# Norm floors taken as a maximum over stored pairs, and unread transposes at four places of the first two batches

## What is computed

```python
EPS = 1e-12
def l2norm(t):
    n = norm(t);  return t / maximum(n, EPS)
def tanh_norm(t):
    n = norm(t);  return tanh(n) * (t / maximum(n, EPS))
q, k, v = l2norm(q), l2norm(k), l2norm(v)
attn = square(relu(q @ k.T))
out  = tanh_norm(attn @ v)
x    = x + out @ Wout
```

## Time and profile before

| | us |
|---|---|
| median of 3 runs | 552.65 (552.19 to 552.93) |
| the profiled execution | 551.87, of which span of the core 549.8 |
| TensorE busy | 527.1 (96%) |
| VectorE busy | 425.2 (77%) |
| ScalarE busy | 371.4 (68%) |
| GpSimd busy | 331.3 (60%) |

### The profile page before, as it was taken

One profiled execution on the slowest core, in us unless ns is written; L12 is line 12 of the kernel. 1 busy time (PEld: TensorE's weight loads), 2 busy tenths in 40 slices (PEclk: granted clock), 3 DMA queues, 4 the chain that ended last, 5 costly groups with the idle time before them and its releaser, 6 DMA issues.

```text
span 549.8 us, 10227 instructions
## 1 busy us (share of the span) xinstructions
PE 527.1 (96%) x3288; PEld 393.9 (72%) x3288; DVE 425.2 (77%) x1004; ACT 371.4 (68%) x682; POOL 331.3 (60%) x280
## 2 busy tenths in 40 slices
PE   8798899999999999898999999999999999999997
PEld 7565557676767666686878878878868878878884
DVE  5877868888978698669769778778769778777765
ACT  5697859687769786644565865865865865755654
POOL 6645919393947584395466655655655655665562
PEclk9899989999999999999999999999999999999999
DMA  7401010101010100660291760870760780771930
GB/s 218 131 2 30 1 30 1 32 1 30 2 31 1 30 2 9 171 148 2 77 209 30 184 153 4 176 156 11 184 151 4 182 175 5 170 159 35 214 83 20
DMA packets 37253, 44.75 MB, mean 81 GB/s; under 512 B 5840, under 2 KB 20304, under 8 KB 37200
## 3 DMA queue, kind: packets, MB, share of 16 engines
q1 hardware_dynamic: 32512, 42.40, 33.3%
q10 hardware_dynamic: 4688, 1.71, 1.3%
HBM read 40.94 MB, written 3.15 MB: 80 GB/s over the span
## 4 chain that ended last, share of the span: by engine, by line
PE 61%; POOL 14%; issue 13%; DVE 6%; ACT 4%; DMA 1%; SPq 0%; POOLq 0%; ACTq 0%; DVEq 0%
PE PS L1245 59%; POOL hl L517 11%; DVE aT L892 2%; ACT v L556 1%; POOL sr L446 1%; ACT rl L581 1%; DMA Osb<-wa_dram 1%; DVE n L871 1%; POOL mrstd L508 1%; POOL rstd L461 1%; DVE nmx L904 1%; ACT sqv L563 0%; POOL fxl L468 0%; DVE hb L1118 0%; PE PS L1338 0%
## 5 line engine op out<-in xcount | busy, mean ns | idle before, releaser
L517 POOL TENSOR_TENSOR hl<-hb,hh 128x512 fp32r<-128x512 f32 x127 | 164.3, 1295 | 129.2 <-ACT hh L735 124.9
L728 ACT ACTIVATE sil<-PS 128x512 f32<-128x512 f32 (+1 forms) x136 | 80.8, 595 | 79.0 <-PE PS L1245 72.4
L1113 DVE TENSOR_TENSOR PS<-sil,PS 128x512 f32<-128x512 f32 x128 | 88.3, 690 | 54.3 <-PE PS L1245 33.0
L1245 PE MATMUL PS<-fxh,wfh 128*128 128x512 f32 x264 | 104.9, 397 | 3.3 <-DVE hb L1118 2.9
L735 ACT ACTIVATE hh<-hb 128x512 fp32r<-128x512 f32 x128 | 80.3, 627 | 35.3 <-DVE hb L1118 33.4
L1245 PE MATMUL PS<-fxl,wfh 128*128 128x512 f32 x264 | 104.1, 394 | 0.0
L1245 PE MATMUL PS<-fxh,wfl 128*128 128x512 f32 x264 | 103.7, 393 | 0.0
L1118 DVE TENSOR_TENSOR hb<-PS,wbc 128x512 f32<-128x512 f32 x128 | 88.5, 691 | 12.9 <-issue 4.2
L892 DVE SCALAR_TENSOR_TENSOR aT<-PS,rl 128x1024 f32<-128x1024 f32 x64 | 75.2, 1216 | 14.7 <-ACT rl L581 14.6
L581 ACT ACTIVATE rl<-PS 128x1024 f32<-128x1024 f32 x64 | 62.8, 1050 | 21.7 <-PE PS L1245 21.7
L436 POOL TENSOR_TENSOR sr<-n2o,half 128x32 f32<-128x32 f32 x7 | 37.9, 5414 | 44.4 <-DVE n2o L899 44.4
(11 more groups left out here) (182 smaller groups left out, 900.1 us busy)
## 6 DMA issues: line engine op xcount, KB each, us to landing
wbc<-w_dram SPq DMA_DIRECT2D x48, 512.0 KB, 11.7
wbc<-w_dram SPq DMA_DIRECT2D x32, 128.0 KB, 3.0
wbc<-w_dram SPq DMA_DIRECT2D x16, 256.0 KB, 4.2
wfs<-wf_dram SPq DMA_DIRECT2D x32, 98.0 KB, 2.2
band_dram<-zero SPq DMA_DIRECT2D x16, 80.0 KB, 1.7
band<-band_dram ACTq DMA_DIRECT2D x4, 320.0 KB, 3.0
X<-x_dram SPq DMA_DIRECT2D x1, 896.0 KB, 8.2
Osb<-wa_dram SPq DMA_DIRECT2D x3, 256.0 KB, 3.8
```

The lines of the kernel that those rows point to most:

```text
L517: g.tensor_tensor(hl[:, n % RING, :], hb[:, n % RING, :], hh[:, n % RING, :].bitcast(F32), ALU.subtract).then_inc(F("hl"), 1)
L728: s.activation(sil[0:rows, n % 2, :], PS[0:rows, G0 + n % 2, :], ACT.Silu).then_inc(F("silu"), 1)
L1113: v_.tensor_tensor(PS[:, bank, :], sil[:, n % 2, :], PS[:, bank, :], ALU.mult).then_inc(F("t"), 1)
L1245: return nc.tensor.matmul(o, w, m, start=start, stop=stop)
```

## The change

Two parts.

First, n2 and nn get a last dimension of 2. GpSimd stores the floor in both places once at the start (two memsets, 576 and 64 elements in each partition); afterwards every sum is written to place 0, and place 1 keeps the floor. The maximum with the floor is then a reduction (maximum) over the innermost pair where it was a tensor_scalar with a constant. This holds for L882, L904, L1012 and L1017. The first reader, `value_norms(0,0)`, waits for the memsets.

Second, a new helper `fill_idle(times, job)` waits until the PSUM bank of the named coming job is free and writes `times` unread transposes of the identity to it. It is called at four places: 6 ahead of `score(0)` (bank of `g 0 2`), 10 ahead of `score(1)` (bank of `qk 1 0`), 8 ahead of `score(5)` (bank of `qk 2 0`), and 10 ahead of `score(9)` (bank of `F 0 0`).

```diff
-            n2 = ab("n2", [P, 3, 2, 3 * H])
+            n2 = ab("n2", [P, 3, 2, 3 * H, 2])
...
-            nn = ab("nn", [P, 2, H])
+            nn = ab("nn", [P, 2, H, 2])
...
             g.memset(ind[:, :, :], 0.0).then_inc(cs("ind0"), 1)
+            g.memset(n2[:, :, :, :, :], NORM_EPS * NORM_EPS).then_inc(cs("floors"), 1)
+            g.memset(nn[:, :, :, :], NORM_EPS).then_inc(cs("floors"), 1)
             inverse_deviation(0)
...
-                g.tensor_tensor(nn[:, :, :], sr[:, :, :], rr[:, q % 3, :, 0:H], ALU.mult).then_inc(A("n"), 1)
+                g.tensor_tensor(nn[:, :, :, 0], sr[:, :, :], rr[:, q % 3, :, 0:H], ALU.mult).then_inc(A("n"), 1)
...
             def value_norms(n, t):
                 dve.wait_ge(A("sqv"), 2 * n + t + 1)
-                v_.tensor_reduce(n2[:, n % 3, t, 2 * H:3 * H], sqv[:, :].rearrange("p (h d) -> p h d", d=DV),
+                if n == 0 and t == 0:
+                    dve.wait_ge(cs("floors"), 2)
+                v_.tensor_reduce(n2[:, n % 3, t, 2 * H:3 * H, 0], sqv[:, :].rearrange("p (h d) -> p h d", d=DV),
                                  AX.X, ALU.add).then_inc(A("n2v"), 1)
...
-                v_.tensor_scalar(nm[:, n % 3, t, :], n2[:, n % 3, t, :], NORM_EPS * NORM_EPS, None, ALU.max).then_inc(A("nm"), 1)
+                v_.tensor_reduce(nm[:, n % 3, t, :], n2[:, n % 3, t, :, :], AX.X, ALU.max).then_inc(A("nm"), 1)
...
-                v_.tensor_scalar(nmx[:, :, :], nn[:, :, :], NORM_EPS, None, ALU.max).then_inc(A("nmx"), 1)
+                v_.tensor_reduce(nmx[:, :, :], nn[:, :, :, :], AX.X, ALU.max).then_inc(A("nmx"), 1)
...
+            def fill_idle(times, *job):
+                bank, k = turns.at[job]
+                after(pe, Z(f"free{bank}"), k - 1)
+                for _ in range(times):
+                    nc.tensor.transpose(PS[:, bank, 0:P], ident[:, :], ident[:, :])
+
...
             group(0, 1)
+            fill_idle(6, "g", 0, 2)
             score(0)
...
+                if b < 2:
+                    fill_idle(10 if b == 0 else 8, "qk", n, 0)
                 if b != 2:
                     score(NG * b + 1)
...
                 if b == 1:
+                    fill_idle(10, "F", q, 0)
                     score(NG * n + 1)
```

More of the change, by code:

```diff
@@ L217, in hybrid_layer @@
         ld = Sems(ctx, nc, "in_x0 in_x in_wv0 in_wv1 in_wq in_wp in_wo in_wf0 in_wf1 in_wf2 in_wf3 in_wf4 in_wf5 in_sd in_gw in_wb in_bb zeroed")
-        cs = Sems(ctx, nc, "id0 id half rid ind0 ind rm rf sel fpad zero sel1 sdz wah wal wph wpl wfh wfl sdh sdl")
+        cs = Sems(ctx, nc, "id0 id half floors rid ind0 ind rm rf sel fpad zero sel1 sdz wah wal wph wpl wfh wfl sdh sdl")
         A = Sems(ctx, nc, "stats mv ve rstd xn xTh vraw sqv n2v n2q nm nm_v rr vi vc0 vc vp S relu a av Oc sqO "
@@ L606, in tanh_norms @@
                 act.wait_ge(A("n"), q + 1)
-                s.activation(th[:, :, :], nn[:, :, :], ACT.Tanh).then_inc(A("th"), 1)
+                s.activation(th[:, :, :], nn[:, :, :, 0], ACT.Tanh).then_inc(A("th"), 1)
             def weight_high(k):
@@ L875, in pair_norms @@
                 dve.wait_ge(*freed("qk", n, t))
-                v_.tensor_reduce(n2[:, n % 3, t, 0:2 * H], sqqk[:, t, :].rearrange("p (h d) -> p h d", d=DK),
+                v_.tensor_reduce(n2[:, n % 3, t, 0:2 * H, 0], sqqk[:, t, :].rearrange("p (h d) -> p h d", d=DK),
                                  AX.X, ALU.add).then_inc(A("n2q"), 1)
@@ L1011, in first_value_floor @@
                 dve.wait_ge(A("n2v"), t + 1)
-                v_.tensor_scalar(nm[:, 0, t, 2 * H:3 * H], n2[:, 0, t, 2 * H:3 * H], NORM_EPS * NORM_EPS, None,
-                                 ALU.max).then_inc(A("nm_v"), 1)
+                v_.tensor_reduce(nm[:, 0, t, 2 * H:3 * H], n2[:, 0, t, 2 * H:3 * H, :], AX.X, ALU.max).then_inc(A("nm_v"), 1)
             def first_pair_floor(t):
                 dve.wait_ge(A("n2q"), t + 1)
-                v_.tensor_scalar(nm[:, 0, t, 0:2 * H], n2[:, 0, t, 0:2 * H], NORM_EPS * NORM_EPS, None,
-                                 ALU.max).then_inc(A("nm"), 1)
+                v_.tensor_reduce(nm[:, 0, t, 0:2 * H], n2[:, 0, t, 0:2 * H, :], AX.X, ALU.max).then_inc(A("nm"), 1)
                 dve.wait_ge(A("nm"), t + 1)
```

## The result

The changed kernel took 548.2 us (median of 6 runs, 546.98 to 550.06) where the kernel before, run beside it, took 552.99 (552.19 to 555.58). The ratio is 0.9909 with a 95% interval of 0.988 to 0.9938: 0.9% faster. The profiled execution took 546.98 us, the lowest of the six, with a span of 545.2, against 551.87 and 549.8. Four executions of 581 to 1756 us (one of the kernel before, two of a3, one of b2) are left out of the ratios of this document.

The account below looks back on a forecast made before the run. It took TensorE as the bound from batch 2 on, with half-clock stretches before. Gains of 0.82 in batch 0 and 2.68 from the end of batch 1 make 3.5 us, giving 549.0 us, range 547.3 to 551.2.

Parts of the forecast that it names:

- The two low stretches: Granted clock at 0.50 from 19.6 to 22.7 us and about 0.50 to 0.55 from 67.3 to 74; fills remove both.
- rival 1: Transposes do not hold the clock, both low stretches stay, only 0.42 us is gained: about 552.2 us; chance 0.07.
- The stands left: TensorE's longest stands left beside the fills, 0.9 us, are shorter than the 1.55 that did not lower the clock.
- Batch 0, 0.82 us: Attend(0) starts at 22.98 instead of 23.80 us, then waiting for GpSimd's v: 0.82 us gained.
- The memsets, 0, at most 0.2: GpSimd's two memsets at the start take 0.75 us and cost 0, up to 0.2 if they held back the first normalisation.
- End of batch 1, 0.42 us: L904 no longer stalls but L908 waits for GpSimd until 63.28 us, so score(9) starts 0.42 us earlier.
- rival 3: The stalls were worth more: L908 does not wait, +0.9 in batch 1, +1.1 in expert pass 0; 547.0 to 547.8; chance 0.12.
- Score(9) to attend(8): At full clock, score(9) to scale_output gains 0.7 us, the second spread 0.2, pairs to attend 1.21, attend(8) itself 0.15.
- Batches 2 to 6, taken as 0: TensorE is the bound there, so freeing VectorE gains probably nothing, at most 1.14 us in the 100 us from 100 to 200.
- Expert pass 0, taken as 0: Without L904's 1.26 us the chain still waits for GpSimd's two hl operations, ending at 250.2: 0 gained, bound 1.1 us.
- Rival 2: Half of it: one low stretch stays or moves, or batches 2 to 6 give part back; 550.0 to 551.4 us; chance 0.14.
- Rival 4: Slower: shifted stands between 220 and 253 us bring new low stretches, 3.4 us each; chance 0.03 for one, 0.05 for more.

Follow-up runs that it names:

- a3: The kernel before plus only the fill of 10 unread transposes ahead of score(1), with the old maxima; ratio 0.9967 to the kernel before.
- b2: The changed kernel with its maxima computed as a two-input tensor_tensor instead of a reduction; ratio 0.9947 to the kernel before.
- a1: The kernel before plus only the floors (stored pairs and reductions), no fills; ratio 0.9947 to the kernel before.
- a4: The kernel before plus only the fill of 10 unread transposes ahead of score(9), with the old maxima; ratio 0.9944 to the kernel before.
- c3: The changed kernel measured again, nothing altered; ratio 0.9912 to the kernel before.
- c4: The changed kernel with memsets on VectorE, the last batch's output_factors one pair later, and VectorE scaling both halves of batch 0's v; 546.97 us, ratio 0.9887.
- a2: The kernel before plus all four fills, with the old maxima; ratio 0.9938 to the kernel before.
- b1: The changed kernel without the fills ahead of score(0) and score(5); ratio 0.9927 to the kernel before.
- b4: The changed kernel with 3 instead of 10 transposes ahead of score(1) and score(9); ratio 0.9948 to the kernel before.

## Why the prediction was right

Forecast 549.0 us (range 547.3 to 551.2), measured 548.2. As a gain that is 3.65 us forecast and 4.8 us measured, so the forecast took about a quarter too little. Step by step:

- *The two low stretches come from TensorE's stands, and unread transposes remove them.* Shown: a1 has both, a3 and a4 each remove their own. The page of the Trainium skill that speaks against transposes (TensorE: Matmul & The Clock Gate, "Part 4: PE-mode transpose") would have made it the 0.42 us of rival 1; the trace contradicts it, as the earlier trace rows did before.
- *The stands left, up to 0.9 us, are shorter than the 1.55 that did not lower the clock.* This step held in the profiled execution of the change and failed in c3, where two stands of 0.77 and 0.83 us close to each other were followed by a fall. The length of a single stand does not decide. (Before the change there was such a neighbour too: the stand "shortly before" that of score(9) is one of 0.48 us ahead of the transposes of the factors at 64.66, which the earlier trace rows does not show.) That the profiled execution of the first comparison was spared is luck in part.
- *Batch 0, 0.82 us, limited by GpSimd's v.* 0.83 measured (4.17 to 3.34), with attend(0) standing for v as forecast; c4 shows that it was v.
- *The memsets, 0, at most 0.2.* Wrong in place. I looked at GpSimd's free time and the first normalisation and not at what VectorE does beside the memset: four tensor_scalars that took 0.6 us longer. On average 0.24 us; 0.29 in the profiled executions, of which c4 shows that the loads can be a part.
- *End of batch 1, 0.42 us.* 0.67 (a1 and the change, 24.59 to 23.92). The mechanism was right: L908 (now L912) took the wait over, 0.90 us. The size was off, because a waiting instruction hides its own time too: the product now ended 0.06 us behind v, where before the reciprocal and the product came after v's end one after the other (63.28 to 63.93). I had counted the reciprocal only. The 1.34 of rival 3 did not come. (The two additions of rival 3, 0.9 and 1.1 us, give 547.0 to 548.1 and not to 547.8; the chances do not hang on it.) The two maxima themselves took 0.25 and 0.16 us, where I had estimated 0.24 and 0.20.
- *Score(9) to attend(8), 0.7 + 0.2 + 1.21 = 2.11 us, and 0.15 in attend(8).* 2.32 and 0.19. Where c3 lost the clock for 3.4 us, the first was 0.93.
- *Batches 2 to 6, taken as 0.* A batch took 26.08 us before and 25.95 after; score(10) to the first stand behind it (206.72 before) got 0.57 us shorter, though TensorE was busy 98.86 of 100 us. The rows show a wait so short that it hardly shows in the busy share. Of before:

```profile
95.94 0.41 DVE L866 TENSOR_TENSOR xTl<-PS,xTh 128x256 fp32r<-128x256 f32 x1
```

```profile
96.46 0.39 PE L1245 MATMUL PS<-FT,sel 32*128 32x256 f32 x2
```

and after:

```profile
91.70 0.42 DVE L868 TENSOR_TENSOR xTl<-PS,xTh 128x256 fp32r<-128x256 f32 x1
```

```profile
92.58 0.39 PE L1247 MATMUL PS<-FT,sel 32*128 32x256 f32 x2
```

  The spread (FT) goes to the bank that VectorE's xTl frees. Before, the spread started 0.11 us behind the end of xTl, now 0.46. On VectorE a long L882 (1.00 us at 91.06) stood ahead of xTl before and is gone now. That this bank is the cause is argued from the turns, not tried; that the gain belongs to the floors is shown, since it is absent with the old maxima (a2) and with two inputs (b2).
- *Expert pass 0, taken as 0.* 0.40 us (25.03 to 24.63 from one stand to the next). L912 took 0.63 us, to the end of the first hl operation, and the cast to Fpad 1.16 us, to the end of the second, where I had named the product between them. So only one operation of the chain is left behind GpSimd's pair, where before three were, and the end did not stay as I had said.

The sum was 3.5 and the span gave 4.6. The main mechanisms were right. Of the three terms that I had set to nought, two were gains (batches 2 to 6 with 0.57 us, expert pass 0 with 0.40) and one a loss (the start, 0.29); the end of batch 1 and score(9) to attend(8) gave 0.25 and 0.21 us more than I had counted. That the time still came so near is partly because the loss at the start took back some of what I had left out. Rival 2 came true in one of two profiles of the change in a milder form (c3). Rival 4 did not show: the clock was 1.00 from 100 to 260 us in all twelve profiles of variants and in that of the change.

## What to carry to other kernels

Read the granted clock by stretch before the busy share: a busy TensorE at 0.50 is a cost that no wait shows. A few unread transposes in the stand that precedes it can buy it back; here they cost nothing as long as they ended before the wait did. Size them to leave little of the stand, and try each place alone: two of the four fills here did nothing. Look at the clock of every execution and not of the profiled one alone, since the fall comes in some and not in others. When a short operation on VectorE is long now and then, look whether it ends with a large operation of GpSimd; here a reduction escaped the wait, but the next product or cast of the chain inherited it.

## What the runs showed of the hardware that I had not expected

- The clock falls at moments of its own. The same stand of about 2 us ahead of score(1) lowered it at its end (before), in the middle of score(1) (a1) or behind it (a4), and in the change it fell once in two profiles after two stands of 0.8 us. A stand of 1.56 us at full clock (b1) did not lower it, one of 1.69 (b4) did, in the profiled execution.
- GpSimd's product on v holds VectorE's operation with two inputs until it ends (L908 of b2, 1.52 us), while its power operation (2.89 us on 16 elements) does not hold it at all: 0.19 us for L912 inside it.
- A cast on VectorE, with one input, is held by GpSimd as well: 1.16 us in expert pass 0 of the changed kernel, where the cast at the end of batch 1 took 0.18.
- A memset by GpSimd, which reads nothing, held VectorE's tensor_scalars for about its length: 1.27 instead of 0.67 us beside a memset of 0.58.
- TensorE can lose 0.1 us per batch at a busy share near 99%.
